# A counting sort with its position sums made in one block, and spread over the steps of the sort

## What is computed

```python
h = layernorm(x)                                   # 6250 x 256
m = silu(concat(h[src], h[dst], w_edge) @ mW1 + mb1)
m = silu(layer_norm(m, ln_g, ln_b) @ mW2 + mb2)
agg = segment_sum(m, src, 6250)
x = x + h + silu(concat(h, agg) @ uW1 + ub1) @ uW2 + ub2
# then the experts' layer on layernorm(x)
```

## Time and profile before

| what | value |
|---|---|
| median of 3 runs | 2843.23 us (2842.95 to 2843.74) |
| the profiled execution | 2843.46 us, span 2841.7 us |
| busy over the span | PE 84%, PEld 72%, DVE 70%, ACT 59%, POOL 45% |
| the sort's matmuls (L927) | first start 121.9 us, last start 550.1 us |
| granted TensorE clock over the span | 0.916 of full |

### The profile page before, as it was taken

The page is one execution under the profiler, slowest core; times in us unless marked ns, Lnnn a source line. Parts: engine busy times, 40 slices in busy tenths (PEclk is TensorE's granted clock), DMA queues, the critical chain, the costliest instruction groups (busy, mean ns, idle before and its releaser), DMA issues. The chain is left out here.

```text
span 2841.7 us, 61657 instructions
## 1 busy us (share of the span) xinstructions
PE 2395.3 (84%) x15142; PEld 2059.0 (72%) x15143; DVE 1999.0 (70%) x6013; ACT 1685.5 (59%) x5927; POOL 1282.3 (45%) x1335
## 2 busy tenths in 40 slices
PE   4388888769999999999999999999999890039990
PEld 4277777647888888888888888888888790038880
DVE  8978888547777777777777877777777664323335
ACT  2766666537777777777777777777776560013330
POOL 2045555625555555555555555555552113644440
PEclk7699989879999999999999999999999995569995
DMA  6010000133233333223332233332243772223338
GB/s 141 3 29 25 27 25 26 33 102 94 86 89 90 89 89 90 87 89 90 90 89 87 88 90 89 90 89 86 88 89 49 214 227 75 93 100 120 123 102 271
DMA packets 151899, 259.47 MB, mean 91 GB/s; under 512 B 32176, under 2 KB 96889, under 8 KB 151448
## 3 DMA queue, kind: packets, MB, share of 16 engines
q0 software_dynamic: 57392, 140.00, 17.8%
q1 hardware_dynamic: 87392, 111.96, 13.0%
q10 hardware_dynamic: 7025, 6.40, 0.7%
HBM read 195.46 MB, written 62.80 MB: 91 GB/s over the span
## 5 line engine op out<-in xcount | busy, mean ns | idle before, releaser
L1033 POOL DMA_INDIRECT work<-dst_half,stage_i x848 | 814.1, 960 | 780.2 <-PE ps L1241 581.0
L1224 PE MATMUL ps<-W2c,work 128*128 128x256 f32 x3392 | 802.3, 379 | 0.0
L1224 PEld LDWEIGHTS ps<-W2c,work 128*128 128x128 f32 x3392 | 612.0, 190 | 70.7
L1059 DVE TENSOR_TENSOR agg<-agg,ps 125x256 f32 x848 | 354.7, 418 | 254.1 <-PE ps L1241 246.4
L1165 ACT ACTIVATE work<-ps 128x512 f32<-128x512 f32 x424 | 252.1, 595 | 353.5 <-PE ps L1241 349.2
L1241 PE MATMUL ps<-work 128*125 128x256 f32 x1696 | 435.2, 379 | 1.3 <-ACT work L1186 1.3
L1180 ACT ACTIVATE work<-work 128x256 f32<-128x256 f32 x848 | 341.6, 404 | 53.5 <-DVE work L1086 49.1
L1215 PE MATMUL ps<-ablk,work 128*128 x2544 | 352.3, 275 | 20.5 <-DVE work L1107 9.8
L1138 DVE SCALAR_TENSOR_TENSOR work<-ps,work,b2c 128x256 f32<-128x256 f32 x848 | 368.7, 477 | 0.0
L513 POOL DMA_INDIRECT edge_records<-stage,work x208 | 229.1, 1101 | 279.8 <-PE ps L927 185.7
L1172 ACT ACTIVATE work<-work 128x256 f32<-128x256 f32 x848 | 340.8, 406 | 3.3 <-issue 3.1
(11 more groups left out here) (277 smaller groups left out, 3313.1 us busy)
## 6 DMA issues: line engine op xcount, KB each, us to landing
work<-tile_sources SPq DMA_DIRECT2D x106, 250.0 KB
work<-routed_tokens SPq DMA_DIRECT2D x53, 257.0 KB
work<-dst_half,stage_i POOLq DMA_INDIRECT x848
routed_tokens<-work SPq DMA_DIRECT2D x26, 514.0 KB
work<-expert_rows SPq DMA_DIRECT2D x25, 320.0 KB, 5.3
update_node_half<-work SPq DMA_DIRECT2D x25, 250.0 KB, 2.2
work<-update_node_half SPq DMA_DIRECT2D x25, 250.0 KB
work<-expert_rows SPq DMA_DIRECT2D x25, 180.0 KB, 6.0
```

The costliest lines, as they stand in the source:

```text
L1033: pool.indirect_dma_start(bg[:, r, u, :], None, dstd, bass.IndirectOffsetOnAxis(ap=stage_i[:, c:c + 1], axis=0)).then_inc(gath[r], 16)
L1059: v.tensor_tensor(d, d, ps[0:NB, (7, 0)[a.mod(2)], u * D:(u + 1) * D], ALU.add).then_inc(agg_add, 1)
L1224: last = t_.matmul(ps[:, 5 + s, u * D:(u + 1) * D], sT[:, a.mod(RT), u, k], W2c[:, k], start=(k == 0), stop=(k == KC - 1))
```

## The change

`position_sums` works on one bank: it is called with a step, waits for that bank alone, and signals after each bank. It runs one group further ahead: before the sort the sums of groups 0 and 1 are made, and during group `g` those of group `g + 2`, one bank behind each of the steps 1 to 4, and the fifth behind step 4 too.

`positions` is cut into `take` (one multiplication), `add_up` (one reduction) and `whole` (the rounding), with a semaphore `pos_ready` of its own. They stand between the parts of the steps.

On POOL, each of the last group's scatters but the first waits for a signal of PE's from the blocks 40 to 45: `u_ps` and `ab_ready` come from the products, `hn_tr` from the turns.

```diff
--- before.py
+++ after.py
@@ -305,6 +305,7 @@
         home_ready = sem("chunk_homes")
         rank_ps = sem("positions_summed")
         rank_taken = sem("positions_taken")
+        pos_ready = sem("positions_added_up")
         lo_ready = sem("low_one_hots")
         lov_ready = sem("sort_operands")
         w_ready = sem("sort_weights")
@@ -510,6 +511,9 @@
                             pool.wait_ge(sorted_ps, m + 1)
                         elif m < NG * NS and k % 3 == 1:
                             pool.wait_ge(ab_ready if m % 2 else hn_tr, m // 2 + 1)
+                        elif g == NG - 1 and k > 0:
+                            t = BK - LATE + (k - 1) // 3
+                            pool.wait_ge((u_ps, ab_ready, hn_tr)[(k - 1) % 3], (t + 1, t + 1, t + 3)[(k - 1) % 3])
                         nc.gpsimd.indirect_dma_start(
                             recd, bass.IndirectOffsetOnAxis(ap=home[:, g, k:k + 1], axis=0),
                             stage[:, i, k * CF:(k + 1) * CF], None).then_inc(scat[i], 16)
@@ -614,17 +618,23 @@
                 pos, hif, lof = spot
                 made = [0]
 
-                def positions(g):
-
-                    dve.wait_ge(rank_ps, g + 1)
-                    for s in range(NS + 1):
-                        if s < NS:
-                            v.tensor_tensor(prod[e, s % 2], one_hot(g)[e, s * SB:(s + 1) * SB, :],
-                                            ps[e, s, 0:SB * BK].rearrange("p (c b) -> p c b", c=SB),
-                                            ALU.mult).then_inc(rank_taken, 1)
-                        if s > 0:
-                            dve.wait_ge(rank_taken, g * NS + s)
-                            link(v.tensor_reduce(out=pos[e, (s - 1) * SB:s * SB], in_=prod[e, (s - 1) % 2], axis=AX.X, op=ALU.add))
+                def take(g, s):
+
+                    m = g * NS + s
+                    dve.wait_ge(rank_ps, m + 1)
+                    wait(dve, pos_ready, m - 1)
+                    v.tensor_tensor(prod[e, s % 2], one_hot(g)[e, s * SB:(s + 1) * SB, :],
+                                    ps[e, s, 0:SB * BK].rearrange("p (c b) -> p c b", c=SB),
+                                    ALU.mult).then_inc(rank_taken, 1)
+
+                def add_up(g, s):
+
+                    dve.wait_ge(rank_taken, g * NS + s + 1)
+                    v.tensor_reduce(out=pos[e, s * SB:(s + 1) * SB], in_=prod[e, s % 2], axis=AX.X, op=ALU.add).then_inc(pos_ready, 1)
+
+                def whole(g):
+
+                    dve.wait_ge(pos_ready, (g + 1) * NS)
                     link(v.tensor_copy(qi[e], pos[e]))
 
                 def split_a():
@@ -675,27 +685,38 @@
                 link(v.tensor_scalar(mv1[e, :, 0], negm[e], -1.0, None, ALU.mult))
                 link(v.tensor_scalar(mv1[e, :, 1], sqs[e], 1.0 / D, None, ALU.mult))
                 v.tensor_scalar(mv1[e, :, 1], mv1[e, :, 1], EPS, None, ALU.add).then_inc(var_ready, 1)
-                positions(0)
+                for s in range(NS):
+                    take(0, s)
+                    if s > 0:
+                        add_up(0, s - 1)
+                add_up(0, NS - 1)
+                whole(0)
                 dve.wait_ge(std_ready, 1)
                 link(v.reciprocal(mv1[e, :, 1], mv1[e, :, 1]))
                 v.tensor_tensor(sqs[e], negm[e], mv1[e, :, 1], ALU.mult).then_inc(hn_coef, 1)
                 split_a()
                 split_b()
                 for g in range(NG):
-                    for s in range(NS - 2):
+                    more = g + 1 < NG
+                    for s in range(NS):
                         operands(g, s)
+                        if more and s < NS - 2:
+                            if s > 0:
+                                add_up(g + 1, s - 1)
+                            take(g + 1, s)
                         node_parts(g * NS + s)
-                    if g + 1 < NG:
-                        positions(g + 1)
-                    operands(g, NS - 2)
-                    node_parts(g * NS + NS - 2)
-                    if g + 1 < NG:
-                        split_a()
-                    operands(g, NS - 1)
-                    node_parts(g * NS + NS - 1)
-                    if g + 1 < NG:
-                        dve.wait_ge(lov_ready, (g + 1) * NS)
-                        split_b()
+                        if more and s == NS - 3:
+                            take(g + 1, NS - 2)
+                        if more and s == NS - 2:
+                            add_up(g + 1, NS - 3)
+                            take(g + 1, NS - 1)
+                            add_up(g + 1, NS - 2)
+                            add_up(g + 1, NS - 1)
+                            whole(g + 1)
+                            split_a()
+                        if more and s == NS - 1:
+                            dve.wait_ge(lov_ready, (g + 1) * NS)
+                            split_b()
 
                 for t in range(BK - LATE - 1, BK - 5):
                     third(t - 1)
@@ -848,24 +869,20 @@
             def _(pe):
                 t_ = nc.tensor
 
-                def position_sums(g):
-
-                    wait(pe, rank_taken, g * NS)
-                    for s in range(NS):
-                        for j in range(s * NS, s * NS + NS):
-                            t_.matmul(ps[:, s, (j - s * NS) * CB * BK:(j + 1 - s * NS) * CB * BK],
-                                      ahead[0:65, j:j + 1].to_broadcast([65, P]),
-                                      tt[0:65, g, :].unsqueeze(1).to_broadcast([65, CB, BK]), start=(j == s * NS), stop=False)
-                    for s in range(NS):
-                        cols = ps[:, s, 0:SB * BK].rearrange("p (c r b) -> p c r b", r=CB, b=BK)
-                        t_.matmul(cols[:, :, 1, :], onesh[e, :],
-                                  one_hot(g)[e, s * SB:(s + 1) * SB, :].rearrange("p (c r) b -> p c r b", r=CB)[:, :, 0, :],
-                                  start=False, stop=False)
-                    for s in range(NS):
-                        last = t_.matmul(ps[:, s, 0:SB * BK], trib[e, :],
-                                         one_hot(g)[e, s * SB:(s + 1) * SB, :].rearrange("p c b -> p (c b)"),
-                                         start=False, stop=True)
-                    last.then_inc(rank_ps, 1)
+                def position_sums(g, s):
+
+                    wait(pe, rank_taken, (g - 1) * NS + s + 1)
+                    for j in range(s * NS, s * NS + NS):
+                        t_.matmul(ps[:, s, (j - s * NS) * CB * BK:(j + 1 - s * NS) * CB * BK],
+                                  ahead[0:65, j:j + 1].to_broadcast([65, P]),
+                                  tt[0:65, g, :].unsqueeze(1).to_broadcast([65, CB, BK]), start=(j == s * NS), stop=False)
+                    cols = ps[:, s, 0:SB * BK].rearrange("p (c r b) -> p c r b", r=CB, b=BK)
+                    t_.matmul(cols[:, :, 1, :], onesh[e, :],
+                              one_hot(g)[e, s * SB:(s + 1) * SB, :].rearrange("p (c r) b -> p c r b", r=CB)[:, :, 0, :],
+                              start=False, stop=False)
+                    t_.matmul(ps[:, s, 0:SB * BK], trib[e, :],
+                              one_hot(g)[e, s * SB:(s + 1) * SB, :].rearrange("p c b -> p (c b)"),
+                              start=False, stop=True).then_inc(rank_ps, 1)
 
                 pe.wait_ge(consts, 14)
                 for g in range(NG):
@@ -910,13 +927,13 @@
 
                 pe.wait_ge(tri_ready, 4)
                 pe.wait_ge(lc_ready, 2)
-                position_sums(0)
+                for g in range(2):
+                    for s in range(NS):
+                        position_sums(g, s)
                 pe.wait_ge(u_in, 16)
                 pe.wait_ge(w_in, 16 * 8)
                 pe.wait_ge(bias_ready, 3)
                 for g in range(NG):
-                    if g + 1 < NG:
-                        position_sums(g + 1)
                     wait(pe, staged, g)
                     for s in range(NS):
                         m = g * NS + s
@@ -932,6 +949,10 @@
                             turn(m // 2)
                         else:
                             products(m // 2)
+                        if g + 2 < NG and s > 0:
+                            position_sums(g + 2, s - 1)
+                    if g + 2 < NG:
+                        position_sums(g + 2, NS - 1)
 
                 turn(BK - LATE)
                 for t in range(BK - LATE, BK - 5):
```

## The result

The changed kernel took 2769.38 us (median of 4, 2767.39 to 2772.13), the kernel before beside it 2843.09: ratio 0.9741, with a 95% interval of 0.9729 to 0.9752. The prediction was 2765, with 2752 to 2780 as the forecast's own range. The profiled execution has a span of 2765.4 us, 76.3 less than before.

The account below looks back on a forecast made before the run. It took DVE and PE waiting in turn in the sort, started by DVE's 6.69 us of positions, as the bound. 2843.2 less 68 (sort) less 10 (paced scatters) gave 2765 us, range 2752 to 2780.

Parts of the forecast that it names:

- The sort, 68 us: Spreading DVE's positions between steps and PE's sums bank by bank ends the sort at 482.4 us, not 550.4.
- DVE's work in a period: In the sort, DVE is busy 44.93 us per two groups and becomes the bound, 2.6 us above PE's 42.3.
- The low clock: In the sort, PE's idle may slow its clock; taken as every second period, making 44.93 + 0.9 = 45.8 us.
- my walk: Step distances followed through a sort period: PE idle once, about 2.5 us, ahead of step 4 of one group.
- The third term: The sort's last group, without positions to make, is set by PE: 17.0 us to its last sort's end.
- DVE's lump: In the sort, DVE's positions in one piece of 6.69 us start the two engines' waiting in turn.
- Part 3, the scatters, 10 us: Behind the sort, scatters delay the store's landing that block 40's copy needs; pacing them saves 10 us, ends nothing and 15.
- the 3 that I had asked for: Sign in the profile after: ACT's idle ahead of block 40's copy, behind the sort, is below 3 us.
- My estimate of the tail without such waits: Behind the sort, blocks 40 to 44 would take some 19 us without waits, where they end 33.9 us after it.
- The first (tail not cured, 2775): The sort evens out, but the store behind it waits for another cause: 2775 us; chance 0.25.
- The second (50.3 us a period): In the sort, part of the engines' waiting in turn stays, 50.3 us a period: about 2803 us; chance 0.18.
- The third: In the sort, many short idles hold PE at the low clock: slower, 2868 us; chance 0.04.

Follow-up runs that it names:

- before_again: The kernel before, unchanged, run once more for a trace on a chip where it took 2812 us; one execution, 2810.03 us.

## Why the prediction was right, and where not

**The sort, 68 us.** Measured 69.2 in the first pair of traces and 70.6 in the second; the last sort ended at 481.25, not 482.4. The mechanism holds: DVE's waits for the copies fell from 50.6 to 7.2 us, DVE is busy for 98% of a period, the granted clock is 0.98, and takes and bank sums wait for nothing. Three terms inside were off, and in part they cancel. DVE's work in a period was 44.19 us, not 44.93. The low clock, for which I had added 0.9 us in every second period, came more seldom. In the second trace, which has no start put down to "remote", PE stands idle once in each period, for 1.2 to 1.9 us where my walk had 2.5. Two of these seven idles are followed by a slow sort:

```profile
206.36 3.08 PE L944 MATMUL ps<-work 125*128 125x104 f32 x20 [1.62 <-ACT work L810]
...
386.84 2.45 PE L944 MATMUL ps<-work 125*128 125x104 f32 x20 [1.87 <-ACT work L810]
...
431.76 3.19 PE L944 MATMUL ps<-work 125*128 125x104 f32 x20 [1.87 <-ACT work L810]
```

The groups with a slow sort took 23.24 and 23.47 us, the others in their place 22.4 to 22.6: 0.7 and 0.9 more, about what I had added. An idle of the same 1.87 us stands ahead of a slow sort and of a quick one, so its length alone does not decide. In the first trace an undisturbed period takes 44.88, with a clock of 1.00. One stretch of 49.08 us (clock 0.93) falls between; in it ACT has two late starts "remote", of 2.33 and 2.10 us, and PE waits for ACT for 2.32 and 2.08. Over 14 groups, from the first rounding at 135.94 us to the last at 454.19, the mean period is 45.46, beside my 45.8. The third term is the last group: from the start of its first sort at 462.13 us to 481.25 it took 19.1 us, not 17.0, in part since PE stands idle 0.70 us behind each of its two turns, as it does before at 547.96 (0.68), which I had read past. The fifteen groups ahead of it ended 3.3 us sooner than I said, so the errors hide each other.

**What the prediction did not see.** It said that DVE's lump "is what starts it", and costed PE's new order at nothing. It costs nothing, but it carries 26 to 28 of the 70 us: DVE's half alone leaves `take` waiting for sums in each group, a wait that the earlier trace rows can't show, since `take` is not late before. It also left out the 18.1 us for which `third` waited.

**Part 3, the scatters, 10 us.** This is the step that failed: "I believe that the scatters hold up the store's landing". The first pair of traces shows 7.2 us less in the tail, and ACT's idle ahead of block 40's copy is 1.30 us, below the 3 that I had asked for, so the profile after alone would have borne it out. The runs do not: with or without pacing the ratio is 0.9741, the store's wait 1.3 us. What had stood for 8.68 us in the earlier trace rows names "remote", not the store, and is a late start of the kind that the traces at 2812 us lack altogether. My estimate of the tail without such waits, 19 us for blocks 40 to 44, was right: in before_again they end 19.4 us behind the sort (567.74 less 548.31), with no pacing. What the late starts come from stays open. So does whether pacing does something on a chip that has them: no unpaced kernel but the kernel before ran there. The tails of the five paced kernels there lie between 41.5 and 45.2 us, and single traces don't tell whether 49.6 stands out from them for a reason. The changed kernel gained 73.7 us there and 72.8 where the tails are equal, so little is left for it. That the total of 2765 came within 4.4 us of 2769.38 is therefore in part luck: 10 of its 78 us stood on a wrong cause, and the 7.2 that came in their place no run ties to the edit.

**The rivals.** The first (tail not cured, 2775) had the right account of the scatters and missed by 6 us, about the 7.2 by which the tail is shorter in the first pair of traces, for a reason that the runs leave open. Behind it stood the rule of the Trainium skill ("DMA: Bandwidth & Descriptors", section on queues, rings and completion order), by which the pacing is worth little; the runs at 2812 us agree (1.0003). The second (50.3 us a period) did not come; the longest stretch of two groups is the one of 49.08. (Its sum, 2843.2 - 33 - 10, gives 2800 and not 2803.) The third needed PE at the low clock; it went from 0.91 to 0.98. The Trainium skill ("TensorE: Matmul & The Clock Gate", the section on psum-queue depth-cycling) spoke for it, and no stretch here shows it: with ten pieces of sums in each period, through the banks in turn, where there were two, PE is granted 1.00 in the periods of 44.88 us. The slow sorts that are left in the two traces behind the first steps stand behind waits for ACT of 1.62 to 2.32 us, not behind the short pieces.

## What to carry to other kernels

Where two engines wait in turn for each other, look for a lump in the row of each, and spread both: here the second was worth 26 to 28 us beside the first's 44, and the waits of the kernel before didn't show it. Before a consumer is spread, ask how many steps it runs ahead of its producer, and place the producer's pieces by that distance; a piece "one group further ahead" that lands at the same place in the row is no lead. A single late instruction in one trace, released by "remote", is no basis for an edit before a second trace shows it again.

## What the hardware showed that I had not expected

The kernel before took 2812 us on two chips and 2844 on others. All six traces at the higher level have starts put down to "remote", and none of the eight at the lower level has one. The largest sum of them for the kernel before in its first trace, whole span; at the other level this instruction has no wait at all:

```profile
DVE agg L1784 <- remote: 34.0, 12, 4.6
```

The spans differ by 33.4 us (2841.7 and 2808.3): 2.1 in the sort, 16.1 in the tail, and 14.4 between the first and the last start of this instruction (133.7 and 119.3 us). So the 34.0 us are not all on the path, and that the late starts make the rest of the difference is argued from their places, not shown. The change's ratio is the same at both levels, 0.9741 and 0.9742.

A GpSimd instruction and one of DVE's that both read SBUF and overlap take longer: 0.64 us became 1.08 and 1.48 became 1.92 in the rows above, 0.44 more for each, as if GpSimd had waited for L666 to end and L668 for GpSimd. The instructions that read one operand from PSUM (L635) or are reductions (L642) stayed at their length, 677 and 668 ns at most. The Trainium skill ("SBUF — State Buffer", section "Who interferes with whom") says that a DVE instruction with two inputs in SBUF contends with a GpSimd instruction that reads SBUF, and that the shared ports are an exclusive lock. The trace agrees, with 12.6 us on L668 for 38 subtractions.
